# A perceiver layer on one core: nine blocks of uneven size in place of eight equal ones

## Time and profile before

| | us |
|---|---|
| median of 3 runs | 1072.03 |
| the profiled execution | 1073.63 |
| its span | 1071.8 |
| DVE busy in the span | 895.7 (84%) |
| PE busy | 950.8 (89%) |
| POOL busy | 858.0 (80%) |
| ACT busy | 759.6 (71%) |

### The profile page before, as it was taken

The page is one execution under the profiler, slowest core; times in us unless marked ns, Lnnn a source line. Parts: engine busy times, 40 slices in busy tenths (PEclk is TensorE's granted clock), DMA queues, the critical chain, the costliest instruction groups (busy, mean ns, idle before and its releaser), DMA issues.

```text
span 1071.8 us, 13076 instructions
## 1 busy us (share of the span) xinstructions
PE 950.8 (89%) x4175; PEld 511.9 (48%) x4210; DVE 895.7 (84%) x1210; ACT 759.6 (71%) x1321; POOL 858.0 (80%) x617
## 2 busy tenths in 40 slices
PE   8786998899988998899898998899898998687886
PEld 7452443445445554545445554446354554432554
DVE  2434797899988999799988999799987999899955
ACT  2346558777797869777796869777896869765634
POOL 1357998998978898799978898799978898899900
PEclk9997999999999999999999999999998999989999
DMA  9813440435042520535042520544042400400000
GB/s 347 323 44 158 166 169 30 168 114 221 21 143 98 214 80 21 197 129 207 20 162 91 202 79 21 197 155 180 2 177 75 143 1 2 177 0 1 1 20 20
DMA packets 21483, 122.63 MB, mean 114 GB/s; under 512 B 3431, under 2 KB 4071, under 8 KB 8872
## 3 DMA queue, kind: packets, MB, share of 16 engines
q1 hardware_dynamic: 15800, 86.99, 22.3%
q10 hardware_dynamic: 5616, 34.81, 8.7%
...
HBM read 114.19 MB, written 7.60 MB: 114 GB/s over the span
## 4 chain that ended last, share of the span: by engine, by line
PE 35%; ACT 22%; DVE 20%; issue 10%; DMA 6%; POOL 5%; SPq 1%; ACTq 0%; DVEq 0%; POOLq 0%
PE bank L1014 17%; PE acc L1014 13%; DVE state L877 11%; ACT decay L665 6%; DMA out<-res 3%; POOL state L598 2%; ACT u L756 2%; ACT soft L651 2%; ACT L665 2%; ACT u L764 2%; DVE raw L860 2%; ACT hid L682 2%; DMA res<-x_scratch 1%; DVE hm L943 1%; DMA brep<-in_w_gateT 1%
## 5 line engine op out<-in xcount | busy, mean ns | idle before, releaser
L877 DVE TENSOR_TENSOR_SCAN state<-decay,state 128x512 f32<-128x512 f32 (+1 forms) x352 | 590.1, 1694 | 45.5 <-ACT decay L665 27.9
L598 POOL TENSOR_TENSOR state<-w,brep 128x512 f32<-128x512 f32 (+1 forms) x352 | 612.6, 1771 | 0.1
L1014 PE MATMUL acc<-state,ident 128*128 128x512 f32 x832 | 409.2, 608 | 16.4 <-DVE state L877 12.0
L665 ACT ACTIVATE decay<-delta,neg_a 128x496 f32<-128x496 f32 x512 | 329.5, 669 | 98.6 <-DVE state L877 97.2
L1014 PEld LDWEIGHTS acc<-state,ident 128*128 128x128 f32 x832 | 147.8, 192 | 166.0 <-issue 114.2
L606 POOL TENSOR_TENSOR state<-state 128x512 f32<-128x512 f32 x96 | 122.2, 1273 | 52.6 <-DVE state L877 51.3
L651 ACT ACTIVATE soft<-x_in,nmr,rstd 128x256 f32<-128x256 f32 x64 | 33.2, 589 | 48.9 <-POOL nmr L564 48.9
L1014 PE MATMUL bank<-xn_t,in_w 128*128 128x512 f32 x128 | 60.1, 603 | 7.5 <-DVE u L1006 5.7
L629 POOL TENSOR_TENSOR w<-delta,u 128x512 f32<-128x512 f32 x32 | 39.9, 1271 | 31.0 <-ACT delta L788 31.0
L692 ACT ACTIVATE sg<-bank,ag 128x512 f32<-128x512 f32 x64 | 43.6, 681 | 29.3 <-PE bank L1014 29.0
L1014 PE MATMUL bank<-out_w,u 128*128 128x256 f32 x256 | 58.0, 382 | 6.7 <-DVE u L868 6.7
...
## 6 DMA issues: line engine op xcount, KB each, us to landing
...
```

What stands on the lines that cost most here:

```text
L598: nc.gpsimd.tensor_tensor(state[g % CPT][:, 0:count, :], w[:, m, :].unsqueeze(1).to_broadcast((P, count, TOK)), brep[:, n:n + count, :], A ...
L665: last = nc.scalar.activation(decay[:, to + i, :, 1:LEN], d, ACT.Exp, scale=neg_a[:, m, n + i:n + i + 1])
L877: nc.vector.tensor_tensor_scan(flat, decay[:, of:of + count, :, :].rearrange("p c q l -> p (c q l)"), flat, 0.0, ALU.mult, ALU.add).then_i ...
L1014: return nc.tensor.matmul(o, l, r, start=first, stop=last)
```

## The change

- The blocks are of 2, 4, 4, 4, 4, 4, 4, 4 and 2 groups (`SIZES`), nine in all; with the phases that fill and drain, eleven phases. All loops, slices and semaphore counts go by the block's own size. A chunk of a small block has 512 or 256 elements.
- In phase 0 block 0's pre (2 groups) runs together with block 1's norm and attention (`AHEAD`, stage "next"), in banks A and B and in buffers of their own (`att_banks`, `att_buffers`). Phase 1 holds the rest of block 1's pre (`SECOND`) and the scan of block 0.
- x has four buffers, and the residual stays in them: the store to DRAM, the load back and `res` are gone.
- The ffn's weights are loaded in five pieces into other buffers, with rows of 256 elements, after block 0's four key loads, x and three key loads of block 1. They are quantised in phase 0, in five pieces; what reuses those buffers waits for it.
- Each kind of phase has its own order table; phases 3 to 7 keep `POST` and `PRE` as they were. `WARM` holds fewer dummy matmuls (those before `x_turn` 12 for 18, before `turn2` 8 for 12).

```diff
+SIZES = (2, 4, 4, 4, 4, 4, 4, 4, 2)
+COUNT = len(SIZES)
+FIRST_GROUP = [sum(SIZES[:b]) for b in range(COUNT + 1)]
...
-KEY_LOADS = (("t", 0), ("t", 1), ("n", 0), ("t", 2), ("n", 1), ("t", 3), ("n", 2), ("n", 3))
+KEY_ORDER = {2: (("t", 0), ("n", 0), ("t", 1), ("n", 1)),
+             4: (("t", 0), ("t", 1), ("n", 0), ("t", 2), ("n", 1), ("t", 3), ("n", 2), ("n", 3))}
...
+def _key_loads():
+    loads, last, turn = [], {}, 0
+    for b, size in enumerate(SIZES):
+        loads.append([])
+        for kind, g in KEY_ORDER[size]:
+            buffer = 3 if (b, kind, g) == (0, "n", 1) else turn % 3
+            turn += buffer < 3
+            loads[b].append((kind, g, buffer, last.get(buffer)))
+            last[buffer] = (b, kind, g)
+    return loads
+KEY_BUFFER = {(b, kind, g): buffer for b in range(COUNT) for kind, g, buffer, _ in KEY_LOADS[b]}
...
+PREPARE = [
+    ("abs_sum", [17, 17, 20, 24, 30]),
+    ("quantise", [9, 22, 27, 60, 65]),
+    ("total", [39]),
+    ("scales", [36]),
...
+FIRST = [
+    ("u_evac", [44, 45, 56, 59]),
+    ("rstd2", [8]),
+    ("add2", [67]),
+    ("x_dbl", [63]),
+    ("exp", [4, 14]),
+    ("xn2", [37]),
+    ("silu", [50, 59, 61, 62]),
+    ("dt", [70, 73, 74, 87]),
+    ("s_max", [2, 8]),
+    ("x1", [33]),
+    ("attn_out", [33]),
+    ("softplus", [80, 84]),
+    ("stats2", [43]),
+    ("times_u", [71, 82, 83, 85]),
...
+AHEAD = [
+    ("s_bias", [49, 63, 76, 87]),
+    ("exp", [31, 47, 62, 71]),
+    ("score", [31, 51, 59, 69]),
+    ("s_max", [24, 54, 69, 85]),
+    ("attend", [52, 69, 73, 87]),
+    ("stats1", [4]),
+    ("xn1", [10]),
...
+SECOND = [
+    ("x1", [9, 15]),
+    ("stats2", [18]),
+    ("mix_in", [27, 31, 43, 45]),
+    ("x_dbl", [69]),
+    ("softplus", [77, 87]),
...
+AGENDA = [
+    _agenda(("prepare", PREPARE), ("pre", FIRST), ("next", AHEAD)),
+    _agenda(("pre", SECOND)),
+    _agenda(("post", POST_FIRST), ("pre", PRE)),
+    *[_agenda(("post", POST), ("pre", PRE))] * (COUNT - 4),
+    _agenda(("post", POST), ("pre", PRE_END)),
+    _agenda(("tail", TAIL), ("post", POST_END)),
+    _agenda(("post", LAST)),
 ]
...
-        x_in = [sb(f"x_in{i}", [P, GROUPS, DIM]) for i in range(2)]
-        res = sb("res", [P, GROUPS, DIM])
+        x_in = [sb(f"x_in{i}", [P, GROUPS, DIM]) for i in range(4)]
...
+        keys = [sb(f"keys{i}", [P, GSEQ * HALVES * KEYS]) for i in range(3)] + [w[:, :, :].rearrange("p m t -> p (m t)")]
...
+        def att_buffers(b):
+            return (xn_1, xn_t_1, q_t_1, z_t_1) if b == 1 else (xn, xn_t, q_t, z_t)
...
+        half = slice(TOK // 2, TOK)
+        ffn_f = [brep[:, STATES // 2:, half], delta[:, :, half], u[0][:, :, half], x_in[3][:, :, :], xn3]
...
+        def att_banks(b):
+            return (A, B) if b == 1 else (D, E)
...
+                    kind, g, _, user = KEY_LOADS[b][k]
+                    if user:
+                        reach(sp, scores_done if user[1] == "t" else z_done, user[0], user[2] + 1)
                     if kind == "t":
-                        sp.dma_start(keys_t[g], t["keys_t"][block_ * GROUPS + g]).then_inc(keys_t_loaded[g % 2], 16)
+                        sp.dma_start(keys_t(b, g), t["keys_t"][FIRST_GROUP[b] + g]).then_inc(keys_t_loaded[g % 2], 16)
                     else:
-                        sp.dma_start(keys_n[g], t["keys_n"][block_ * GROUPS + g]).then_inc(keys_n_loaded[g % 2], 16)
-                        if block_ == 0:
+                        sp.dma_start(keys_n(b, g), t["keys_n"][FIRST_GROUP[b] + g]).then_inc(keys_n_loaded[g % 2], 16)
+                        if b == 0:
                             sp.wait_ge(prep_p, PREP_P)
-                        sp.dma_start(keys_l[g % 2][0:GSEQ, :], t["keys_l"][block_ * GROUPS + g])\
+                        else:
+                            reach(sp, z_done, *((b, g - 1) if g >= 2 else (b - 1, SIZES[b - 1] - 1 + g)))
+                        sp.dma_start(keys_l[g % 2][0:GSEQ, :], t["keys_l"][FIRST_GROUP[b] + g])\
                             .then_inc(keys_n_loaded[g % 2], 16)
 
-                if post and pre:
-                    reach(sp, out_stored, j - 2, 0)
-                    sp.dma_start(res[:, :, :], t["x1_scratch"][j - 2]).then_inc(res_loaded, 16)
+                def load_tokens(b):
+                    if b >= 4:
+                        reach(sp, out_stored, b - 3, 0)
+                    if b == 3:
+                        sp.wait_ge(quantised, 4)
+                    reach(sp, moments_ready[0], b - 1, SIZES[b - 1])
+                    for to, at, of in pairs(b):
+                        sp.dma_start(x_in[b % 4][:, to, :], t["x"][at][:, of, :]).then_inc(x_loaded, 16)
+                    for k in range(3):
+                        load_keys(b, k)
                 if pre:
                     if not scan:
-                        for k in range(3):
-                            load_keys(j, k)
+                        for k in range(len(KEY_LOADS[0])):
+                            load_keys(0, k)
                         load_mixer_weights()
+                        load_tokens(1)
                         load_ffn_weights()
-                    for k in range(3, len(KEY_LOADS)):
+                        for k in range(3, len(KEY_LOADS[1])):
+                            load_keys(1, k)
+                    for k in range(3, len(KEY_LOADS[j])) if j >= 2 else ():
                         load_keys(j, k)
-                    if j + 1 < BLOCKS:
-                        reach(sp, x1_stored, j - 1, 16)
-                        sp.dma_start(x_in[1 - par][:, :, :], t["x"][j + 1]).then_inc(x_loaded, 16)
-                        for k in range(3):
-                            load_keys(j + 1, k)
-                    if j < BLOCKS - 2:
-                        reach(sp, res_biased[1], j, 1)
-                        sp.dma_start(t["x1_scratch"][j], x_in[par][:, :, :]).then_inc(x1_stored, 16)
-                    reach(sp, x_dbl_ready, j, 1)
-                    reach(sp, b_loaded[BG - 1], j - 1, 16)
-                    sp.dma_start(t["b_scratch"], x_dbl[DROWS:XROWS, :]).then_inc(b_stored, 16)
+                    if 1 <= j < COUNT - 1:
+                        load_tokens(j + 1)
+                    if j:
+                        reach(sp, x_dbl_ready, j, 1)
+                        reach(sp, b_loaded[BG - 1], j - 1, 16)
+                        sp.dma_start(t["b_scratch"][:, 0:SIZES[j] * P], x_dbl[DROWS:XROWS, 0:SIZES[j] * P])\
+                            .then_inc(b_stored, 16)
                 if post:
-                    reach(sp, out_ready, j - 2, GROUPS)
-                    sp.dma_start(out[j - 2], (res if pre else x_in[par])[:, :, :]).then_inc(out_stored, 16)
+                    b = j - 2
+                    reach(sp, out_ready, b, SIZES[b])
+                    for of, at, to in pairs(b):
+                        sp.dma_start(out[at][:, to, :], x_in[b % 4][:, of, :]).then_inc(out_stored, 16)
 
...
+                to = (gate_q[:, :, :].rearrange("p h (r c) -> p (h r) c", c=DIM),
+                      up_q[:, 0, :].rearrange("p (r c) -> p r c", c=DIM),
+                      up_q[:, 1, :].rearrange("p (r c) -> p r c", c=DIM),
+                      down_q[:, 0:KT // 2, :], down_q[:, KT // 2:KT, :])[i]
+                n = (0, 1, 1, 2, 2)[i]
...
+                    groups, tok = SIZES[b], SIZES[b] * P
+                    if not scan and b != 1:
...
+                        if b == 1 and g == BG // 2:
+                            act.wait_ge(quantised, 1)
...
-                        if g == 0 and pre:
-                            reach(dve, res_loaded, b, 16)
-                        if g == 0 and not pre:
-
+                        if g == 0:
                             reach(dve, res_biased[1], b, 1)
-                        r = (res if pre else x_in[par])[:, 2 * g:2 * g + 2, :].rearrange("p g d -> p (g d)")
...
```

723 lines of the change are left out of this document (445 added, 278 removed).

## The result

The changed kernel takes 1068.23 us (median; 1066.35 to 1071.14) beside 1075.73 us (1070.94 to 1080.22) for the kernel before on the same chip: a ratio of 0.9934, 95% interval 0.9918 to 0.9950. The forecast was 1055. The change is faster by 0.7% or 7.5 us, less than half of the 17 that were forecast. The profiled execution has a span of 1066.5 us, against 1071.8; that of the kernel before lay 2 us under its median, so the two spans are only 5.3 us apart.

What follows compares the result with a forecast made beforehand. Full phases were bound by DVE, PE and POOL within 6% of each other, the ends by 141 us of latency. Phase terms 74, 66, 112, 588.5, 109, 73 and 32 sum to 1054.5 us of span, giving 1055, range 1046 to 1063.

Steps and rivals of the forecast that it cites:

- The end of phase 0: First scan forecast at 74 us where it was at 91.9, a gain of 18; range 68 to 85.
- step (a): Phase 0's DMAs: 13.7 MB take 40 us, 42 with the start, so x1 lands near 45.
- (b): Phase 0, block 0's mixer: stats2 to first scan takes 23 us for 34.1, ending at 70 to 75.
- (c): Phase 0 on POOL: quantising from 49 takes 19.4 us, then add2, two w and the first product; ends at 73.5.
- are early already: Key loads on SP's queue, behind 12 dropped transfers of 512 KB: taken as early, the queue's change costed at nothing.
- Phase 8: Small pre: DVE work 103 us at a 94% share, forecast 109 (105 to 114) for 120.1 before.
- Phases 3 to 7: DVE's residual add loses its 2.3 us wait per phase: 117.7 each, 588.5 together, gain 12, bounds 0 and 15.
- Rival 1: Full phases: the 2.3 us wait may come back as PE or ACT waits, giving 1067 us; chance 0.18.
- Phases 1, 2 and 9, the end: Forecast 66 us (60 to 75), 112 (108 to 116), 73 (65 to 82) and 32 (30 to 35).
- Rival 2: Phase 0 doesn't shrink: block 1's key loads go singly, last exp and softplus at 88, total 1071 us; chance 0.12.
- Rival 3: Small-scan phases 1 and 9: TensorE's clock falls and PE binds, slower, 1083 us or more; chance 0.08.
- The sign of the whole: Faster, 1055 us: gains of 18 and 17 at the ends, 12 in the middle, paid with 30 for an eleventh phase.

Runs made afterwards that it cites:

- e2: Changed kernel with SP issuing the ffn's weights ahead of block 1's key loads; ratio 0.9929 to the kernel before.
- e6: Changed kernel with block 1's norm and attention put back into phase 1; ratio 1.0151 to the kernel before.
- e10: Changed kernel with B's loads first, ffn's weights before block 1's keys, block 1's query and first scores behind attn_out, full-phase table in phase 8; ratio 0.9802.
- e7: Changed kernel with both single edits, B's loads ahead of block 2's and the full phases' table cut to two groups in phase 8; ratio 0.9791.
- e1: Changed kernel with SP issuing block 2's x and first key loads only after block 0's loads of B have landed; ratio 0.9870.
- e14: e10 with block 1's query behind the weights' total, dummies before turn2 gone, its first exp between xn2 and evac2; 1049.99 us, ratio 0.9766.
- e4: Changed kernel with phase 8 taking the full phases' pre table, cut to two groups; ratio 0.9860 to the kernel before.
- e5: Kernel before with only the residual kept on chip in four x buffers, no store or load back; 1057.5 and 1056.9 us, ratios 0.9827 and 0.9834.
- e13: e10 with block 1's query and first exp further back, mixer's weights at step 34, block 1's second key load behind block 0's scores; ratio 0.9881.

## Why the prediction was wrong, point by point

**The end of phase 0 (+12.7), step (a), (b) and (c).** Three terms, in order:

- *x1 at 50.3, not 45 (+5.3).* Step (a) fails. It divided the bytes by the DMAs' rate and so took them as never idle: all landed by 42. But SP stood for 12 us at a key load of block 1, and the ffn's weights behind it landed from 42.3 to 48.1. DVE's five sums of them, 2.29 + 4 x 1.22 = 7.2 us, run from 42.4 to 50.1, and x1 stands behind them in DVE's order. PE's side ended at the same time: block 1's query, `kb` and scores are 7.4 us of PE ahead of attn_out (e2). The forecast listed block 1's attention among what was added and priced only its exps on ACT. Taking away one of the two gave nothing (e2, e6); both gave x1 at 43.5 (e10).
- *From x1 to the scan 31.4, not 29 (+2.4).* 86.7 less 50.3 is 36.4, of which 5.0 are B's; in e7, where B is out of the way, x1 came at 49.9 and the scan at 81.5, 31.6 later. Steps (b) and (c) met at 74 with POOL's product as the last link. In e1, e7 and e14 the last link is ACT's decay, behind a table load of 1.28 us and block 1's steps on ACT. Without block 1's work (e6) the same stretch took 27.9 us, 26.6 of them from stats2, for which (b) took 23. So the half mixer alone took more than it was priced at, at a granted clock of 0.81 against 1.00 in e7; how much of that is the clock, no run separates.
- *B's loads (+5.0).* Not in the forecast, which wrote of the key loads that they "are early already". They were too early: x and the first key load of block 2 were issued between B's store (70.1) and B's loads (from 74.2), the second key load among them. e1 shows the 5.0.

Step (c) was right in the length of quantising (19.3 us from 53.9 to 73.2, forecast 19.4) and wrong in its start. Its sum is also off: 49 + 19.4 + 4.1 is 72.5, not 73.5.

**Phase 8 (+8.3).** The forecast took DVE's work and the usual share of it. The order was not the usual: `PRE_END` spaces two groups over the steps in its own way, and DVE, 104.5 busy of 117.3, waited 6.4 us for `sg`. `PRE` cut to two groups gave 112.5 (e4) and 110.2 (e7), within the forecast's 105 to 114. The kernel shows that phase 8 has a table of its own; the forecast took no account of it.

**Phases 3 to 7 (-4.3): the mechanism right, the term mis-sized.** Rival 1, the wait that only changes its name, fell: e5 alone took 120.1 to 116.4. The measured time lies next to that rival's 1067, and by luck only: the full phases did not stay at 120, and phases 0 and 8 overran by 21 us together. The gain of 16.3 is beyond even the bound of 15. The forecast argued from phase 2 of before, 117.7 without a wait for `res`. That phase gave 1.3 us as well once the stores were gone. In it DVE's wait for `sg` fell from 1.3 to 0.2 and the granted clock rose from 0.99 to 1.00; why, no run separates.

**Phases 1, 2 and 9, the end.** 63.3 for 66, 111.9 for 112, 74.8 for 73: within the ranges given. The end took 28.4 for 32, under its range of 30 to 35: from y_last to the end of the last maximum it is 20.0 us, where the forecast had 24 (26.4 before, less 2.4), since it took off two groups' norm and scaling alone. The stretch from the first statistics to the first `sg` alone shrank from 13.8 to 8.7 us. The small scans cost what the line said: 6.9 us more of scan for the forecast's 6. The Trainium skill, "VectorE: DVE Perf Modes", section "The TRN2 errata — SBUF-src ops pay a fixed extra latency per instruction", says that each small tile pays a fixed cost again. The trace agrees: 678 ns for 256 elements, where half of the 1212 ns for 512 would be 606.

**Rival 2** (phase 0 doesn't shrink, the last exp and softplus held by key loads) named the right phase and the right queue, but the wrong place: SP's standing at a key load made the ffn's weights and x1 late, not the exps. delta was there at 77, w at 78.4, and B's loads and PE's order did the rest. **Rival 3** fell: the granted clock was 0.88 and 0.89 in phases 1 and 9, above the 0.8 named, with PE busy 53.8 of 63.3 and 56.2 of 74.8. The Trainium skill, "TensorE: Matmul & The Clock Gate", section "HAM oscillation — how this bites in real kernels", would have each gap pay again; the trace agrees that gaps pay (e13's `kb` at 0.50, and three stretches at 0.50 in each of the phases 1 and 9), but they were too few to bind. The stand-still that the forecast read from the earlier trace rows was also longer than its 4 us: PE's rows of the kernel before have a gap of 7.8 us there, up to 938.6.

**The sign of the whole.** The forecast split the gain as 12 from the middle and 5 net from the uneven blocks. Shown: 18 to 19 from the residual (e5), and 9 to 12 lost by the uneven blocks as they were ordered. With the order mended they do gain: e14 spends 464.6 us outside phases 3 to 7, 5.8 less than e5, which is about the 5 forecast. Of phase 0, 3.7 us (77.7 against 74) stay: x1 comes at 41.9, 3.1 sooner than forecast, but from there to the first scan it takes 35.8 us and not 29. Of that 7.3 us lie between x1 and turn2 (4.8 in the changed kernel), where block 1's query still stands; for the rest no run names the cause.
